# A decoder layer on one core: the self-attention half rebuilt around two heads per pass, masked diagonal blocks and one-bank row maxima

## The chip, the core and the metric

The program runs on 1 core of one Trainium2 chip. The metric is the device time of one execution in microseconds. The engines: TensorE (PE; its weight loads are PEld in the profile) multiplies, VectorE (DVE), ScalarE (ACT) and GpSimd (POOL) compute on rows of 128 partitions, SyncE (SP) issues the DMAs. TensorE writes to PSUM, which has 8 banks of 512 fp32 columns.

## What is computed

One pre-norm decoder layer on x of shape (1, 1024, 128): self-attention, cross-attention to a context of 6404 rows with an added mask, and an FFN with weights and activations rounded to FP4 blocks. Only the self-attention is touched by the change, and the turning of the context that is done on its way:

```python
q = x @ W_q ; k = x @ W_k ; v = x @ W_v
latent_kv = (k + v) @ W_down_kv
k_rec = (latent_kv @ W_up_k)  # 16 heads of 8
v_rec = (latent_kv @ W_up_v)
scores = einsum('bhqd,bhkd->bhqk', qh, k_rec) / sqrt(d)
decay = exp(-0.01 * abs(t[:, None] - t[None, :]))
attn = softmax(scores * decay)
out = einsum('bhqk,bhkd->bhqd', attn, v_rec) @ W_o
```

## The kernel before

All code is written out per engine, with semaphores between the engines; each engine executes its instructions in the order written, so the order of the text is the order of the work.

**Operands.** A head has only 8 dimensions, and the scores are wanted at fp32 accuracy from bf16 matmuls. So each of q and k is split into PARTS = 3 bf16 parts, and 9 products of parts are stacked as 72 rows of one contraction. `|i-j|` in the decay is taken apart: exp(-a(i-j)) is a factor of the query times a factor of the key, right below the diagonal; its inverse is right above it. So there are four operands, QL and KL ("lower"), QU and KU ("upper"). Three more rows (72 to 74) carry minus the row maximum of the query in three parts, against rows of ones. The parts are computed by ScalarE and VectorE, stored to DRAM (`key_parts`, `query_parts`) and loaded back in the stacked form, three loads per operand (`load_operand`, L286 to L296). There are NB = 3 operand buffers for the NG = 4 groups of HG = 4 heads.

**Maxima.** The softmax needs the row maximum before the exponential. One unit is 128 queries of a head against all 1024 keys: two matmuls (`max_unit`, L868 by way of the helper `mm`) into two banks, then one VectorE instruction that multiplies by the decay table and reduces to a maximum (L671). 16 units make a half group (4 heads, 512 queries); 128 units in all. After each half group the 16 columns of maxima are turned on TensorE (`max_rows`, L930), split into three parts on VectorE (`shift_split`, L702 to L705), and written by 6 DMAs into the shift rows of the operand (`load_shift`, L304). Units run ahead of the loop: 16 + MAX_LEAD = 25 are done in a fill before it, and the others go two to a block.

**Scores.** A block is one pair of a query half (512 columns) and two key tiles, 4 heads: four units of 128 keys by 512 queries in banks 0 to 2 in turn. Even units hold a diagonal 128x128 piece, in which neither factor form is right; it is multiplied without shift rows, VectorE multiplies it by the table `diagT` (L747), and TensorE then adds the shift with a matmul against `ones_rows` (`shift_diag`, L958). Odd units are wholly on one side. ScalarE takes the exponential of a unit (L537). P·V is four matmuls side by side, one head in each 32 columns of the array, summing in bank 3 over the 8 blocks of a half group (`pv`, L969). 64 blocks in all. This line sets TensorE's order in a block (s = shift, A and B = a maximum unit each, D, N, d, n = scores):

```python
ORDER = "s0 A D1 PV s1 N1 d0 B n0".split()
```

After every 8 blocks the scores of the next half group wait for its shift rows (`nxt`).

**SyncE** issues in this order: ones, parts of KL and QL, their loads, parts of QU and KU, their loads, then group by group operands and shift rows; the context (`mem`, 3.3 MB, L335 and L336) after two groups; the cross-attention's masks after the last P·V.

**Other work in the loop.** VectorE computes the scales of the FFN weights in blocks 8 to 10 (`weight_scales`). In the last blocks TensorE turns the context (`mem_tiles`, L981) and VectorE splits it into a high and a low part (`mem_parts`, L692 and L694). After the loop comes the cross-attention for 8 tiles of 128 queries, then the FFN, pipelined; they begin at 291 us.

Of the kernel before, what the change touches and what calls it, by code (L numbers as in the profile page):

```python
# [15 lines left out]
P = 128  # L16
# [7 lines left out]
SHIFT_ROW = 72  # L24
MATH_ROWS = 72
FULL_ROWS = SHIFT_ROW + PARTS
HG = 4
# [3 lines left out]
def decoder_layer(nc, x, ctx, mask, w_q, w_k, w_v, w_o, w_down_kv, w_up_k, w_up_v,  # L31
# [27 lines left out]
    MAX_LEAD = 9  # L59
    MEM_BLOCK = (NG * NH * UNITS - UNITS - MAX_LEAD + 3) // 2  # L60
    EARLY_BLOCK = NG * NH * (S // P) - 3
    SCALE_BLOCK = NT
# [4 lines left out]
    with ExitStack() as stack:  # L67
# [8 lines left out]
        SLOTS = 2 * PARTS - 1  # L76

        k_scratch = nc.dram_tensor("key_parts", [2, SLOTS, HD, HEADS, S], BF16, kind="Internal").ap()
# [4 lines left out]
        wq_sb = sb("wq_sb", [P, D]); wk_sb = sb("wk_sb", [P, D]); wv_sb = sb("wv_sb", [P, D])  # L83
        wo_sb = sb("wo_sb", [P, D]); wdn_sb = sb("wdn_sb", [P, DL])
        wuk_sb = sb("wuk_sb", [DL, D]); wuv_sb = sb("wuv_sb", [DL, D])
        xw_sb = sb("xw_sb", [P, D]); xwT = sb("xwT", [P, D]); xb_sb = sb("xb_sb", [P, 1])
        half_neg = sb("half_neg", [P, NT])
        ones_rows = sb("ones_rows", [P, P], BF16)
# [8 lines left out]
        row_max = sb("row_max", [P, NG * NH * UNITS])  # L97
        shift_r = sb("shift_r", [UNITS, 1, P])
        shift_parts = sb("shift_parts", [UNITS, PARTS, P], BF16)
        diagT = sb("diagT", [P, P])  # L100
# [6 lines left out]

        memT_lo = sb("memT_lo", [P, NK * P], F32R)
        qc = sb("qc", [P, 2, P])
# [5 lines left out]
        NB = 3  # L115
        OPW = HG * S
        with ExitStack() as self_stack:
            def sb1(name, shape, dt=F32):
                return self_stack.enter_context(nc.sbuf_tensor(name, shape, dt))
            ops = [sb1(f"operands_{b}", [P, 4, HG, S], BF16) for b in range(NB)]  # L120
            probs = sb1("probs", [P, 2 * HG, BANK])
            oT = sb1("oT", [P, NG * NH, BANK])
            v_ext = sb1("v_ext", [P, NT, HEADS, VW])
            decay = sb1("decay", [P, 2 * S - P])
        OPB = 4 * HG * S // 2
        logits_0 = sb("logits_0", [P, S2])
        pT = sb("pT", [P, 3, BANK]); sb("pad_0", [P, OPB - S2 - 3 * BANK])
        mem = sb("mem", [P, NK, D])
        fa = sb("fa", [P, 4, FF]); sb("pad_1", [P, OPB - NK * D - 4 * FF])
        memT_hi = sb("memT_hi", [P, NK * P], F32R)  # L130
        fb = sb("fb", [P, 4, FF]); sb("pad_2", [P, OPB - NK * D - 4 * FF])
        logits_1 = sb("logits_1", [P, S2]); sb("pad_3", [P, 16 * BANK - S2])
# [5 lines left out]
        def operand(buf, which):  # L138
            return ops[buf][:, which, :, :]
# [4 lines left out]
        def queries(buf, which, half):  # L144
            return ops[buf][:, which, :, :].rearrange("p h n -> p (h n)").rearrange(
                "p (a h n) -> p a h n", a=NH, h=HG)[:, half, :, :]
# [25 lines left out]

        ones_src = xqT[:, 0:P // 2].bitcast(BF16)
        xT = ops[2][:, 2, 0:2, :].rearrange("p h n -> p (h n)").bitcast(F32)
# [3 lines left out]
        scaled = [probs[:, 4, :], probs[:, 5, :]]  # L178
        wq_dh, wuk_dh = probs[:, 6, 0:D], probs[0:DL, 6, D:2 * D]
        wkvT, wdnT = probs[:, 6, 2 * D:3 * D], probs[0:DL, 6, 3 * D:4 * D]  # L180
        w_lift, w_rec = probs[:, 7, 0:2 * D], probs[:, 7, 2 * D:4 * D]
        parts_sb = ops[1][:, 0:PARTS, :, :].rearrange("p w h n -> p (w h) n").rearrange("p (w a) n -> p w a n", w=4)
        iota_i = ops[2][:, 0, 0:4, :].rearrange("p h n -> p (h n)")[:, 0:2 * (2 * S - P)].bitcast(I32)
        iota_d = ops[2][:, 1, 0:4, :].rearrange("p h n -> p (h n)")[:, 0:2 * (2 * S - P)].bitcast(I32)
# [1018 lines left out]
```

## Time and profile before

| | |
|---|---|
| median of 3 runs | 584.27 us (576.2 to 584.42) |
| the profiled execution | 584.69 us, of which the span of the core is 583.0 us |
| mean granted TensorE clock | 0.893 of 2.4 GHz |
| busy: TensorE, VectorE, ScalarE, GpSimd | 504.6, 403.5, 301.2, 102.3 us |
| preparation and fill of maxima | 0 to 66 us |
| self-attention loop | 66 to 291 us |
| cross-attention and FFN | 291 to 583 us |

All times are microseconds in one profiled execution unless another unit is given. An engine's name with "idle before" says how long it stood and whose instruction released it. PEclk is the granted TensorE clock as a share of 2.4 GHz; 0.5 is the lower of its two levels, 1.2 GHz.

### The profile page before, as it was taken

What the parts mean: (1) busy time and instruction counts of PE and PEld (TensorE: products, weight loads), DVE (VectorE), ACT (ScalarE), POOL (GpSimd) and SP (SyncE); (2) the same over time, 40 slices, a digit from 0 to 9 for tenths busy, and PEclk for the clock granted to TensorE, in tenths of its full rate; (3) what the DMA queues carried; (4) which work ended last, traced back from release to release, by engine and by line L of the source; (5) the groups of instructions that cost most, each with busy time, mean ns of one, the idle gap of its engine ahead of it and who ended that gap; (6) DMA issues with size and microseconds to landing.
All of it is one profiled execution on the core that took longest, in us unless ns stands there. A gap on an engine that the chain in (4) does not pass through costs nothing.

```text
span 583.0 us, 9028 instructions
## 1 busy us (share of the span) xinstructions
PE 504.6 (87%) x3222; PEld 321.0 (55%) x3222; DVE 403.5 (69%) x1026; ACT 301.2 (52%) x601; POOL 102.3 (18%) x119
## 2 busy tenths in 40 slices
PE   7258999889999999999887998989899898989953
PEld 6101233223233333345365997978789797878851
DVE  3889869879698988889377345756646566664443
ACT  4710256447475757677716572726446372638420
POOL 6020000980000000000034322221312212210000
PEclk9755579879698989899989998989989998999985
DMA  2690535307000800001057524323232422400000
GB/s 65 191 276 22 102 66 103 65 2 161 5 1 3 226 3 1 3 3 37 1 190 224 146 83 117 115 72 110 87 110 86 146 87 79 139 15 6 1 6 5
DMA packets 20727, 46.04 MB, mean 79 GB/s; under 512 B 4470, under 2 KB 9786, under 8 KB 20106
## 3 DMA queue, kind: packets, MB, share of 16 engines
q1 hardware_dynamic: 19930, 44.74, 27.9%
q8 instruction: 26, 0.43, 0.3%
q0 software_dynamic: 224, 0.54, 0.3%
q10 hardware_dynamic: 528, 0.18, 0.2%
q14 instruction: 19, 0.16, 0.1%
HBM read 40.39 MB, written 4.72 MB: 77 GB/s over the span
## 4 chain that ended last, share of the span: by engine, by line
PE 66%; DVE 25%; issue 3%; DMA 2%; ACT 2%; POOL 0%; SPq 0%; DVEq 0%; ACTq 0%; POOLq 0%
PE banks L868 43%; PE banks L969 11%; DVE banks L671 8%; PE banks L1101 6%; PE banks L958 3%; DVE logits L775 3%; DVE fa L811 1%; DMA operands<-query_parts 1%; DVE qc_lo L729 1%; PE banks L981 1%; DVE fa L810 1%; DVE fa L806 1%; DVE f_small L802 1%; ACT probs L537 1%; DMA x_sb<-in_x 1%
## 5 line engine op out<-in xcount | busy, mean ns | idle before, releaser
L537 ACT ACTIVATE probs<-banks 128x512 f32<-128x512 f32 x256 | 139.1, 596 | 117.4 <-PE banks L958 115.3
L868 PE MATMUL banks<-operands 72*128 72x512 bf16 (+5 forms) x704 | 158.3, 360 | 14.6 <-DMA operands<-query_parts 8.0
L671 DVE CUSTOM_DVE_ANT_0 banks<-banks,decay 128x1024 f32<-128x1024 f32 x128 | 156.5, 1228 | 15.1 <-PE banks L868 11.2
L868 PEld LDWEIGHTS banks<-mem,pT 128*128 128x128 f32 (+1 forms) x816 | 107.9, 195 | 7.7
L868 PE MATMUL banks<-mem,pT 128*128 128x128 f32 (+1 forms) x816 | 111.5, 279 | 0.0
L868 PEld LDWEIGHTS banks<-operands 72*128 72x128 bf16 (+1 forms) x704 | 62.0, 104 | 82.1 <-DVE row_max L671 24.5
L775 DVE CUSTOM_DVE_ANT_0 logits<-banks,mring 128x512 f32<-128x512 f32 (+1 forms) x102 | 67.4, 668 | 46.6 <-PE banks L868 23.2
L559 ACT ACTIVATE pT<-banks 128x512 f32<-128x512 f32 (+1 forms) x104 | 60.4, 581 | 52.6 <-PE banks L1101 52.6
L969 PE MATMUL banks<-probs,v_ext 128*32 128x512 f32 x512 | 76.6, 673 | 0.7 <-ACT probs L537 0.7
L430 POOL TENSOR_SCALAR mring<-mring 128x1024 f32<-128x1024 int32 (+1 forms) x55 | 52.7, 959 | 90.3 <-DMA mring<-in_mask_BxSxS_ik 88.1
L868 PE MATMUL banks<-memT_hi,qc_hi 128*128 128x512 f32 (+1 forms) x104 | 50.4, 485 | 17.7 <-DVE cmax L775 17.7
L1101 PE MATMUL banks<-ident,logits 128*128 128x128 f32 (+1 forms) x408 | 63.5, 279 | 0.0
L549 ACT ACTIVATE logits<-logits,neg_max 128x1024 f32<-128x1024 f32 (+1 forms) x56 | 58.8, 1051 | 6.4 <-DVE neg_max L782 6.4
L958 PEld LDWEIGHTS banks<-operands,ones_rows 75*128 75x128 bf16 x128 | 12.5, 98 | 83.8 <-DVE banks L747 67.9
L747 DVE TENSOR_TENSOR banks<-banks,diagT 128x128 f32<-128x128 f32 x128 | 40.6, 317 | 21.1 <-PE banks L868 21.0
L1101 PEld LDWEIGHTS banks<-ident,logits 128*128 128x128 f32 (+1 forms) x408 | 49.4, 143 | 4.0 <-issue 2.0
L868 PE MATMUL banks<-memT_hi,qc_lo 128*128 128x512 f32 (+1 forms) x104 | 41.4, 398 | 0.0
L868 PE MATMUL banks<-memT_lo,qc_hi 128*128 128x512 f32 (+1 forms) x104 | 41.1, 395 | 0.0
L958 PE MATMUL banks<-operands,ones_rows 75*128 75x128 bf16 x128 | 29.8, 233 | 12.5 <-DVE banks L747 12.3
L420 POOL TENSOR_TENSOR rstd<-mv,half_neg 128x1 f32<-128x1 f32 x16 | 8.8, 552 | 146.3 <-DVE mv L817 83.2
L868 PEld LDWEIGHTS banks<-memT_hi,qc_hi 128*128 128x128 f32 x104 | 20.7, 199 | 20.4 <-DVE cmax L775 19.7
L430 POOL TENSOR_SCALAR mask<-mask 128x1024 f32<-128x1024 int32 x1 | 1.0, 1046 | 135.5 <-DMA mask<-in_mask_BxSxS_ik 135.5
(162 smaller groups left out, 456.0 us busy)
## 6 DMA issues: line engine op xcount, KB each, us to landing
mring<-in_mask_BxSxS_ik SPq DMA_DIRECT2D x47, 512.0 KB, 3.5
operands<-key_parts SPq DMA_DIRECT2D x24, 192.0 KB
operands<-query_parts SPq DMA_DIRECT2D x24, 192.0 KB
key_parts<-operands SPq DMA_DIRECT2D x10, 256.0 KB, 3.5
query_parts<-operands SPq DMA_DIRECT2D x4, 384.0 KB, 4.7
mring<-in_mask_BxSxS_ik SPq DMA_DIRECT2D x8, 130.0 KB, 2.1
operands<-shift_parts SPq DMA_DIRECT2D x48, 4.0 KB, 1.7
x_sb<-in_x SPq DMA_DIRECT2D x1, 512.0 KB, 4.4
```

The costliest lines, as they stand in the source:

```text
L420: pool.tensor_tensor(rstd[:, t:t + 1], mv[:, t, 1:2], half_neg[:, t:t + 1], ALU.pow).then_inc(done, 1)
L430: pool.tensor_scalar(src.bitcast(F32), src, -1.0, -NEG, ALU.add, ALU.mult).then_inc(s_ma, 1)
L537: act.activation(probs[:, (gb % 2) * HG + h, :], PS[:, u % 3, :], ACT.Exp).then_inc(s_p, 1)
L549: act.activation(y, y, ACT.Exp, bias=neg_max[:, t:t + 1], accum_out=esum[:, t, e:e + 1]).then_inc(s_e, 1)
L559: last = act.activation(pT[:, n % 3, 0:o], PS[:, 2 + n % 2, 0:o], ACT.Copy)
L671: dve.tensor_tensor_reduce(out=rows, in0=rows, in1=decay[:, off:off + S], scale=1.0, scalar=-3.0e38, op0=ALU.mult, op1=ALU.max, accum_out= ...
L747: dve.tensor_tensor(PS[:, u % 3, c0:c0 + P], PS[:, u % 3, c0:c0 + P], diagT[:, :], ALU.mult).then_inc(s_dd, 1)
L775: dve.tensor_tensor_reduce(out=logits_sb(t)[:, k0:k0 + kw], in0=PS[:, logits_bank(n), 0:kw], in1=mk, scale=1.0, scalar=-3.0e38, op0=ALU.ad ...
L868: return pe.matmul(o, a, b, start=start, stop=stop)
L958: pe.matmul(PS[:, u % 3, d0:d0 + P], ones_rows[0:FULL_ROWS, :], queries(gb // BLKS % NB, QL, half)[0:FULL_ROWS, h, d0:d0 + P], start=False ...
L969: last = pe.matmul(PS[h * VW:(h + 1) * VW, 3, :], v_ext[:, kt, g * HG + h, :], probs[:, (gb % 2) * HG + i, :], start=(b % NT == 0), stop=( ...
L1101: last = pe.transpose(PS[0:kw, 2 + n % 2, j * P:(j + 1) * P], logits_sb(t)[:, k * P:k * P + kw], ident[:, :])
```

## The change

It rebuilds the self-attention and leaves the mathematics of the cross-attention and the FFN.

1. **Operands.** 6 products of parts in place of 9: 48 rows, then 3 shift rows at 48, in runs given by `RUNS`. Heads h and h+2 of a group lie in the two row halves of the array (rows 0 and 64, `ROW_HALF`), so one slot of work is one matmul per half. Two operand buffers. Loading a group takes 36 DMAs instead of 12.
2. **Diagonal blocks.** The VectorE multiplication and the shift matmul are gone. The lower form is computed over the diagonal piece too; a bf16 matmul of an identity against a table of 0 and -1e30 (`side_mask`) adds -1e30 on the wrong side (L1101). A fifth slot per pair of blocks computes the four heads' diagonal pieces in the upper form, with the other side masked (`diag_scores`, L1114), and its P·V is added apart (`pv_diag`, L1139).
3. **Maxima** from operands of their own (`max_queries`, `max_keys`, 32 rows, four row quarters), in pieces of one bank (512 keys) in a ring of banks 5 to 7: 256 pieces, 44 of them in the fill, then 8 to a pair of blocks. Per piece one VectorE instruction; the two halves of 16 rows' maxima are joined by one more (`join_pieces`).
4. **Shift rows.** GpSimd splits the joined maxima (`max_split`), TensorE turns the three parts at once as bf16 (L1053), ScalarE copies them out (`take_shift`), SyncE writes them with 12 DMAs per half group (L375).
5. **Loop.** 32 pairs of 5 slots. A slot's scores are two banks (0-1 or 2-3), and ScalarE takes one exponential over both (128x1024; 128x512 for the diagonal slot). P·V in two halves of 256 columns, bank 4.
6. **Context.** Loaded right after the weights, turned in the fill (steps from unit 6 on) into banks 0 to 3; ScalarE copies the high part, TensorE subtracts it by a matmul with a negative identity (`mem_rest`), ScalarE copies the low part. VectorE and the loop have none of it.
7. **Parts.** Low parts and the upper operands' remainders move from VectorE to GpSimd, the FFN scales ahead of the first maximum piece.

The diff, cut to its core:

```diff
-SHIFT_ROW = 72
-MATH_ROWS = 72
+ROW_HALF = 64
+RUNS = ((0, 3, 0), (24, 2, 1), (40, 1, 2))
+SHIFT_ROW = 48
...
-    MAX_LEAD = 9
+    SLOTS = 5
+    MAX_LEAD = 6
+    ROWS_LATE = 4
+    FILL = HG_PIECES + MAX_LEAD * NH
...
+            sp.dma_start(mem[:, 0:NKF, :], ctx[0, 0:NKF * P].rearrange("(t p) d -> p t d", p=P)).then_inc(s_mem, 16)
...
+            for i in range(3):
+                weight_scales(i)
...
-                    dve.tensor_tensor(PS[:, u % 3, c0:c0 + P], PS[:, u % 3, c0:c0 + P], diagT[:, :],
-                                      ALU.mult).then_inc(s_dd, 1)
...
+                dve.tensor_tensor_reduce(out=rows, in0=rows, in1=decay[:, off:off + BANK], scale=1.0, scalar=-3.0e38,
...
+            def scores(n, j):
...
+                mm(PS[:, bank + 1, :], keys(g % NB, side[1], h)[:, kt * P:(kt + 1) * P], queries(g % NB, side[0], half, h))
...
+                mm(PS[:, bank, d0:BANK], keys(g % NB, KL, h)[:, ks], queries(g % NB, QL, half, h)[:, d0:BANK])
...
+                pe.matmul(PS[:, bank, d0:d0 + P], ident_b[:, :], side_mask[:, 0, :], start=False, stop=True,
+                          skip_group_check=True).then_inc(s_st, 1)
...
+                        act.activation(probs[:, gb % 2 * HG + i:gb % 2 * HG + i + 2, :],
+                                       PS[:, q % 2 * 2:q % 2 * 2 + 2, :], ACT.Exp).then_inc(s_p, 1)
...
+            pe.wait_ge(s_mlo, NC)
+            for n in range(PAIRS):
+                scores(n, 0)
+                if n > 0:
+                    pv(2 * n - 1, 0)
+                max_turn(8 * n)
+                max_turn(8 * n + 1)
+                scores(n, 1)
...
+                diag_scores(n)
+                pv(2 * n, 1)
+                max_turn(8 * n + 7)
```

**TensorE, one block before**, early in the first group. `ones_rows` with `operands` is the shift matmul, `operands` alone scores or a maximum unit (the unit waits for `max_scores_taken`), `v_ext` P·V:

```order
L958 MATMUL banks<-operands_0,ones_rows 128x128 [waits diag_decayed]
L868 MATMUL banks<-operands_0 128x512 [waits max_scores_taken]
L868 MATMUL banks<-operands_0 128x512
L868 MATMUL banks<-operands_0 128x128 [waits probs_ready]
L868 MATMUL banks<-operands_0 128x256
L868 MATMUL banks<-operands_0 128x128
L969 MATMUL banks<-probs,v_ext 32x512 [waits probs_ready]
L969 MATMUL banks<-probs,v_ext 32x512 x3
L958 MATMUL banks<-operands_0,ones_rows 128x128 [waits diag_decayed]
L868 MATMUL banks<-operands_0 128x512 [waits probs_ready]
```

**TensorE, the last pair before a half group ends, after the change**: from the end of its slot 0 on. `max_keys` is a maximum piece, `qc,xqT` the mask matmul (these two tiles hold the masks and the bf16 identity meanwhile), `xqT,max_parts` the turning of the split maxima:

```order
L1053 MATMUL banks<-xqT,max_parts 48x128 [waits max_scores_taken,max_split]
L1001 MATMUL banks<-max_keys_1,max_queries_1 128x512 [waits max_scores_taken] x2
L1001 MATMUL banks<-operands_0 128x512 [waits probs_ready]
L1001 MATMUL banks<-operands_0 128x128
L1001 MATMUL banks<-operands_0 128x384
L1101 MATMUL banks<-qc,xqT 128x128
L1128 MATMUL banks<-probs,v_ext 32x256 x4
L1001 MATMUL banks<-max_keys_1,max_queries_1 128x512 [waits shift_rows_ready]
...
L1114 MATMUL banks<-qc,xqT 128x256 x2
L1128 MATMUL banks<-probs,v_ext 32x256 x4
L1001 MATMUL banks<-max_keys_1,max_queries_1 128x512 [waits max_scores_taken]
L1001 MATMUL banks<-operands_0 128x512 [waits probs_ready,shift_loaded_1]
```

The scores of the pair after it wait for the shift rows that were turned one pair earlier. Scores, masks, P·V and pieces alternate in each slot; before, a shift matmul and P·V stood among scores.

**SyncE before**, from the first query parts to the operand loads:

```order
L277 DMA query_parts<-operands_1 128x3x512 [waits lo_ready]
L277 DMA query_parts<-operands_1 128x3x512
L296 DMA operands_0<-key_parts 24x4096 [waits scratch_written_1]
L296 DMA operands_0<-key_parts 24x4096 x2
L296 DMA operands_0<-query_parts 24x2x2048 [waits scratch_written_0]
L296 DMA operands_0<-query_parts 24x2x2048 x2
```

**SyncE after**, from the first keys on, the context first; `xqT` is the source of the ones, and `xn` holds the copied shift rows:

```order
L312 DMA mem<-in_ctx_1024 128x50x128 [waits kv_weights_loaded,weights_loaded,x_loaded]
L313 DMA mem<-in_ctx_1024 4x128
L317 DMA key_parts<-operand_parts 128x1024 [waits hi_ready]
L317 DMA key_parts<-operand_parts 128x1024 [waits mid_ready]
L323 DMA query_parts<-operand_parts 128x2x512 [waits mid_ready]
L323 DMA query_parts<-operand_parts 128x2x512
L353 DMA max_keys_0<-key_parts 8x2x512 [waits scratch_written_1]
L353 DMA max_keys_0<-key_parts 8x2x512 x15
L361 DMA max_queries_0<-query_parts 16x2x1024 [waits scratch_written_0]
L361 DMA max_queries_0<-query_parts 16x2x1024 x7
...
L375 DMA operands_0<-xn 1x8x128 [waits shift_rows_ready]
L375 DMA operands_0<-xn 1x8x128 x11
```

The context load now stands ahead of every store of parts, and all of the first group's loads and those of the next group's maxima stand ahead of the first shift rows.

## Rows read from the trace of the kernel before

**Rows 1.** The page's first part: busy us (share of span) xinstructions.

```profile
PE 504.6 (87%) x3222; PEld 321.0 (55%) x3222; DVE 403.5 (69%) x1026; ACT 301.2 (52%) x601; POOL 102.3 (18%) x119
```

**Rows 2.** Stretches: each engine's busy time (instructions), PEclk, DMA share, GB/s.

```profile
0.00:66.00 66.00, 42.25 (x138) 15.56 (x139) 52.06 (x106) 19.27 (x33) 13.17 (x20) 0.66 0.46 130
66.00:80.00 14.00, 13.61 (x53) 4.68 (x52) 8.52 (x18) 6.25 (x12) 0.00 (x0) 0.51 0.73 137
...
102.00:110.00 8.00, 5.44 (x39) 1.87 (x38) 7.79 (x21) 3.78 (x8) 7.42 (x8) 1.00 0.58 119
...
147.00:160.00 13.00, 12.37 (x52) 4.08 (x56) 7.92 (x18) 5.27 (x10) 0.00 (x0) 0.61 0.02 3
160.00:176.00 16.00, 16.00 (x120) 6.23 (x112) 15.37 (x37) 11.92 (x24) 0.00 (x0) 1.00 0.01 2
...
291.00:583.00 292.00, 252.23 (x1735) 224.76 (x1735) 166.07 (x513) 139.90 (x304) 61.01 (x70) 0.94 0.30 91
```

**Rows 3.** TensorE's timeline: start, duration, line, xcount, [idle before <-releaser].

```profile
33.44 1.86 PE L868 MATMUL banks<-operands 72*128 72x512 bf16 x4 [7.96 <-DMA operands<-query_parts]
```

**Rows 4.** SyncE's timeline: DMA issues, as start, duration, line, xcount.

```profile
15.98 2.70 SPq L272 DMA_DIRECT2D key_parts<-operands  x5
...
23.01 2.11 SPq L296 DMA_DIRECT2D operands<-key_parts  x3
...
56.32 3.78 SPq L304 DMA_DIRECT2D operands<-shift_parts  x6
60.15 1.60 SPq L282 DMA_DIRECT2D operands<-xqT  x2
...
93.50 1.18 SPq L296 DMA_DIRECT2D operands<-key_parts  x3
...
189.04 9.36 SPq L336 DMA_DIRECT2D mem<-in_ctx  x1
```

**Rows 5.** TensorE's timeline in an undisturbed block.

```profile
159.62 1.06 PE L969 MATMUL banks<-probs,v_ext 128*32 128x512 f32 x8
...
161.77 0.22 PE L958 MATMUL banks<-operands,ones_rows 75*128 75x128 bf16 x1
161.83 0.82 PE L868 MATMUL banks<-operands 72*128 72x512 bf16 x4
162.57 1.06 PE L969 MATMUL banks<-probs,v_ext 128*32 128x512 f32 x8
163.57 0.23 PE L958 MATMUL banks<-operands,ones_rows 75*128 75x128 bf16 x1
```

**Rows 6.** Groups, 80 to 250 us: xcount | busy us, mean ns | idle before, releaser.

```profile
L671 DVE CUSTOM_DVE_ANT_0 banks<-banks,decay 128x1024 f32<-128x1024 f32 x95 | 116.4, 1226 | 11.3 <-PE banks L868 7.6
L537 ACT ACTIVATE probs<-banks 128x512 f32<-128x512 f32 x191 | 103.8, 596 | 64.4 <-PE banks L958 62.9
...
L747 DVE TENSOR_TENSOR banks<-banks,diagT 128x128 f32<-128x128 f32 x96 | 31.0, 323 | 11.5 <-PE banks L868 11.5
```

**Rows 7.** Waits, 80 to 250 us: who for whom, us, times, longest.

```profile
PEld banks L958 <- DVE banks L747: 52.7, 59, 2.0
```

**Rows 8.** ScalarE's timeline around a handover of shift rows.

```profile
147.90 1.08 ACT L537 ACTIVATE probs<-banks 128x512 f32<-128x512 f32 x2 [1.59 <-PE banks L958]
151.98 1.09 ACT L537 ACTIVATE probs<-banks 128x512 f32<-128x512 f32 x2 [2.99 <-PE banks L958]
```

**Rows 9.** VectorE's timeline in the cross-attention.

```profile
341.12 0.69 DVE L775 CUSTOM_DVE_ANT_0 logits<-banks,mring 128x512 f32<-128x512 f32 x1 [0.28 <-DVE cmax L775]
...
341.74 0.35 DVE L725 TENSOR_SCALAR xn<-x_sb,mv,rstd 128x128 f32<-128x128 f32 x1
```

**Rows 10.** ScalarE's timeline when the small weights have arrived.

```profile
7.59 0.43 ACT L466 ACTIVATE probs<-wuk_sb 32x128 f32<-32x128 f32 x1 [1.13 <-DMA xb_sb<-in_L_xattn_b]
```

**Rows 11.** The tile of split maxima: duration of its DMAs' issue, min/median/max ns, and landing.

```profile
L304 SPq DMA_DIRECT2D operands<-shift_parts x48: 502/589/1372, 56.3 to 260.6; - x48
...
DMA to landing us min/median/max: 1.7/1.7/2.8
```

## What the change should do to the time: the prediction

> **What bounds the kernel now.** I read the page's first part, then a table of stretches, then the waits and the engine timelines inside the self-attention loop. The page alone misleads: TensorE is busy 87% of the span [rows 1], but two different programs share that figure. From 291 us on the kernel is cross-attention with TensorE busy 252 of 292 us [rows 2], and the change leaves that part as it is. So the question is what happens in the first 291 us. These split into a preparation (first matmul of a maximum at 33.44 us, waiting for query operands [rows 3]), a fill of 25 maximum units, and 64 blocks of the loop, from the first exponential at 66 us to the last P·V at 291 us, where I cut the stretches of [rows 2].
>
> In an undisturbed stretch of the loop (160 to 176 us) TensorE is busy all the time and VectorE 15.37 of 16 us [rows 2]; P·V starts at 159.62 and again at 162.57, so a block takes 2.95 us [rows 5]. VectorE ends it: per block two maximum units of 1.23 us and two diagonal multiplications of about 0.32 us [rows 6] make 3.1 us, less some overlap of neighbours. TensorE waits for those multiplications for 52.7 us [rows 7], ScalarE for TensorE's shift matmuls for 62.9 us [rows 6]. 64 x 2.95 = 189 us, yet the loop takes 225. The other 36 us are a cold start (clock 0.51 from 66 to 80 us [rows 2]), the FFN weight scales put among the blocks, and seven handovers of shift rows, after which ScalarE waits 1.59 and 2.99 us and the clock falls: 0.61 over 147 to 160 us [rows 2, 8].
>
> **The change, part by part, for one pair of blocks (5.9 us before without handovers).**
>
> VectorE: the diagonal multiplications and the shift split go. Eight one-bank maxima replace four of two banks. The nearest operation, the masked logits of 128x512 from PSUM, starts at 341.12 and the next instruction at 341.74 [rows 9]: 0.62 us, so 8 x 0.62 = 5.0 us. One join of 128x16 per 32 pieces is nothing beside that.
>
> ScalarE: four exponentials of 1024 columns and one of 512. A 512 one lasts 596 ns, two in a row take 1.08 us [rows 6, 8]; a double one lies between 0.98 (one start saved) and 1.1 us (none saved). I take 1.0: 4.6 us.
>
> TensorE: columns at 2.4 GHz. A 512-column bf16 matmul is 0.213 us. Scores: two heads in two row halves, 0.213 us if they run side by side, plus the mask of 128 columns, 0.053: four slots, 1.07 us. Diagonal slot: 0.11 + 0.21 for the two masks of 256 columns, 0.32. P·V in fp32: two passes of two, 4 x 512 columns = 0.853 us per block whether halved or not: 1.71. P·V of the diagonal parts 0.11 more (a quarter of the columns, half as long each pass). Maxima: eight pieces in five groups, 5 x 0.213 = 1.07 us, since a group of two sits in two row quarters. Together 4.3 us. Side by side is not shown for rows here; for columns it is: the eight records of one P·V last 1.06 us together [rows 5], where one after another they would need 4 x 0.853.
>
> But TensorE changes its tiling between these. The order shows, in each of five slots, scores (51 rows), mask (128 rows), P·V (32 columns), pieces (32 rows): four changes, 20 per pair. The price is in the rows: from the shift matmul at 161.77 to P·V at 162.57 are 0.80 us for 128+512+512+384+128 = 1664 columns, 0.69 us; from P·V at 162.57 to the next at 163.57 are 1.00 us for 0.85 [rows 5]. So about 0.1 us for going in and 0.1 for coming out, though before it happens twice in a block. 20 x 0.1 = 2.0 us: TensorE needs 6.3 us per pair, more than VectorE. With a short wait for the third bank I take 6.4. The bounds: 5.1 (changes free, VectorE sets it) and 8.0 (nothing side by side: 4 x 0.21 + 0.11 + 3 x 0.21 = 1.6 more).
> The Trainium skill says in "TensorEngine Tiling (Array Packing)", Key Properties, that changing the tiling mode, not only the tile, drains TensorE. The trace agrees for a column tiling, at 0.1 us. Were it free for row tilings, the pair would take 5.1 us, and the sum would be near 577.
>
> Pieces end after 26.5 pairs (212 pieces are left after the fill, eight a pair). The last 5.5 pairs lack them and one change per slot: 6.3 - 1.07 - 0.5 = 4.7 us, ScalarE 4.6; I take 4.9. Loop: 26.5 x 6.4 + 5.5 x 4.9 = 197 us.
>
> Start of the loop. SyncE is the path here. The context load is put ahead of everything else: it can be issued when the small weights are in, 7.6 us [rows 10], and a load behind it held SyncE for 9.36 us [rows 4], so SyncE is free at 17.8 us, 2 us after the key parts are there. The stores then follow its 3.3 MB: key and query parts are back at about 23.5 us (23.0 before [rows 4]). From there SyncE issues: 24 loads for the maxima, 8 of ones, 8 stores, 36 operand loads, 24 loads for the maxima of the next group, 12 shift rows. Spacings: loads 0.41 us (three in 1.18 plus the gap), ones 0.80, stores 0.5 (five in 2.70), shift rows 0.63 (six in 3.78) [rows 4]. Sum: 9.8 + 6.4 + 4 + 14.8 + 9.8 + 7.6 = 52.4, and 1.7 for the last to land [rows 11]: 77.5 us. First maximum at 23.5 + 9.8 + 2 = 35.5 us, two later than before. The fill (44 pieces of 0.62 us, from the sixth unit on with 16 steps of transposes and remainder matmuls on TensorE) ends between 62 us (full clock) and 80 us (half clock) and lies beside the queue. I take 77.5, between 70 and 82. ScalarE's 26 copies of 0.6 us, GpSimd's remainders and the scales, now ahead of the first maximum, are covered by the same queue; uncovered, the scales' 5 us would come ahead of the first maximum.
>
> Handovers. The rows of half-group x are turned in slot 0 of pair 4x-1 and wanted by the first scores of pair 4x: one pair, 6.6 us with the transpose. The chain in it: 1.2 us to the transpose, 0.8 to ScalarE's copy behind an exponential, then 12 DMAs, where before there were 6 with four blocks (12 us) of lead, then 1.7 us landing [rows 11]. The nearest row is 0.63 us a DMA with 16 pieces each; these have 8, the loads of long rows take 0.41. I take 0.55: 2.0 + 11 x 0.55 + 1.7 = 9.75, so TensorE stands for 3.1 us (1.6 at 0.41, 4.0 at 0.63). Behind it wait P·V of the last block, then all pieces, so VectorE too; nothing catches up since TensorE bounds. After such stops before, the clock fell for some 3.4 us; TensorE then loses half, 1.7 us. 7 x 4.8 = 34 us.
>
> Sum: 77.5 + 197 + 34 + 292 (from 291 us to the end, unchanged) = 600.5 us of span, + 1.7 for what lies around it (584.69 against 583.0): 602, which I keep, since the median of 584.27 us is only 0.4 below the profiled execution.
>
> **Rivals.** A measurement can tell about 2%, 11.7 us, from no change.
> 1. Faster: the issue of short DMAs is cheaper than any row here (0.3 us or less). Then the queue ends near 68 us, the fill sets 70, the handover chain is 2.0 + 3.3 + 1.7 = 7.0 and hides but for 0.4 us: 70 + 197 + 3 + 292 + 1.7 = 564. For it: each DMA carries half the pieces. Against: 0.589 us is the median of the shift rows, 0.502 the least [rows 11].
> 2. No change: shift rows at 0.41 us and the clock holds through stops of 1.6 us: 75 + 197 + 11 + 292 + 1.7 = 577, with half of the clock drops 583. A free change of tiling comes to 577 as well (34 us less in the pairs, 9 more in the handovers, whose lead is one pair). For it: over 102 to 110 us TensorE was busy 5.44 of 8 us and the clock stayed at 1.00 [rows 2].
> 3. Much slower: the row halves do not run side by side. Pair 8.0 us, last pairs 5.9, stops 1.5 + 1.7: 77.5 + 244 + 22 + 292 + 1.7 = 637. Against: columns do.
>
> **How the numbers follow.** Forecast 0.46, rival 1 0.22, rival 2 0.20, rival 3 0.12. The forecast's own range is 584 to 613 (stops of 1.6 to 4.0 us, loop start 70 to 82). For 8 in 10 the range takes in rival 1 and most of rival 3: 560 to 632. Faster by over 2%: rival 1 and a bit, 0.24. Within 2%: rival 2 and the forecast's lower end, 0.26. Slower: 0.50.
>
> **What would show it.** Right: a pair at 6.3 to 6.6 us with TensorE never idle and VectorE waiting for it; 0.1 us between matmuls of different tilings; scores of heads h and h+2 starting within some 10 ns; SyncE issuing without a pause from 24 to 76 us; at seven places the first scores waiting for DMA operands<-xn, 2 to 4 us. Wrong: pairs at 5 us with VectorE full; shift DMAs under 0.4 us; first exponential before 70 us; two heads' matmuls 0.2 us apart.

## The result, and the profile after

The changed kernel takes 711.15 us (median of 4 runs, 709.95 to 712.27), the kernel before 583.11 us (median of 4); the ratio is 1.2225 with a 95% interval of 1.2123 to 1.2327. The forecast was 602 us, the range ended at 632. The sign was right, the size was not: the time is 109 us above the forecast and 79 us above the end of the range.

The stretches of the changed kernel show where. Columns as in [rows 2].

```profile
0.00:66.00 66.00, 44.13 (x189) 24.20 (x189) 48.83 (x134) 33.13 (x60) 51.85 (x60) 0.77 0.56 162
66.00:77.50 11.50, 0.60 (x1) 0.10 (x1) 2.11 (x8) 0.05 (x1) 4.31 (x6) 0.51 0.16 43
80.00:376.00 296.00, 294.96 (x1806) 71.46 (x1804) 150.67 (x427) 127.51 (x144) 4.97 (x24) 0.50 0.08 21
380.50:387.00 6.50, 4.87 (x61) 1.74 (x59) 0.00 (x0) 4.58 (x5) 0.00 (x0) 1.00 0.02 3
412.00:708.00 296.00, 255.30 (x1779) 226.35 (x1778) 166.99 (x513) 141.83 (x307) 60.88 (x70) 0.94 0.30 90
```

The last row is the cross-attention: from the end of the last P·V (415.5 us, before 292.0) it is 293 us to the end, before 291. So the change left it as it was, and nearly all of the excess is in the loop, from the first exponential at 78.4 to 415.5 us: 337 us, where it was 226. The third row has the cause in it. For 296 us TensorE is busy almost without a gap (294.96 us), and its granted clock is 0.50, the lower level, all that time. Before, the clock was 1.00 in the undisturbed stretches of the loop [rows 2]. It rises in this trace at 380 us; the last maximum pieces were multiplied from 374.4 to 375.0 us. The page's second part shows it at a glance, the busy share and the clock in tenths, 17.7 us a digit:

```profile
PE   7097699999999999999998987989898989898873
...
PEclk9658555555555555555556799999999999999995
```

The first line misleads: TensorE reads 9 in almost every slice of the loop, nothing looks idle. The second tells it.

The pace can be read off ScalarE's timeline. The first exponential of a pair of blocks starts at 132.50 and the next pair's at 143.75: 11.25 us a pair, where 6.4 were forecast.

```profile
132.50 1.02 ACT L689 ACTIVATE probs<-banks 128x1024 f32<-128x1024 f32 x1 [1.72 <-PE banks L1101]
134.82 1.02 ACT L689 ACTIVATE probs<-banks 128x1024 f32<-128x1024 f32 x1 [1.29 <-PE banks L1101]
...
143.75 1.02 ACT L689 ACTIVATE probs<-banks 128x1024 f32<-128x1024 f32 x1 [1.72 <-PE banks L1101]
```

In TensorE's timeline the same work, a slot without pieces, stands at both clocks, first at the lower level and then, after the rise, at the higher:

```profile
376.29 0.60 PE L1001 MATMUL banks<-operands 51*128 51x512 bf16 x3
376.83 0.29 PE L1101 MATMUL banks<-qc,xqT 128*128 128x128 bf16 x1
377.05 1.08 PE L1128 MATMUL banks<-probs,v_ext 128*32 128x256 f32 x8
...
381.24 0.39 PE L1001 MATMUL banks<-operands 51*128 51x512 bf16 x3
381.56 0.23 PE L1101 MATMUL banks<-qc,xqT 128*128 128x128 bf16 x1
381.72 0.64 PE L1128 MATMUL banks<-probs,v_ext 128*32 128x256 f32 x8
382.29 0.39 PE L1001 MATMUL banks<-operands 51*128 51x512 bf16 x3
```

A slot without pieces takes 382.29 - 381.24 = 1.05 us at 2.4 GHz: 0.32 from scores to mask, 0.16 to P·V, 0.57 to the next scores. Its columns alone need 0.213 + 0.053 + 0.427 = 0.69, so three changes of tiling cost 0.36 us, 0.12 each. From 376.29 to 377.05 at 1.2 GHz are 0.76 us for 0.427 + 0.107: two changes, 0.11 each. The change from P·V to what follows is 0.57 - 0.427 = 0.14 at 2.4 GHz and 1.01 - 0.853 = 0.16 at 1.2 GHz (377.05 to 378.06). So a change costs about the same time at either clock.

So the question for the runs: why does a TensorE that is always busy not get its higher clock? Theory A: the content, small tiles that fill too little of the array. Theory B: history, the clock was lost at the wait before the loop (66 to 77.5 us, second row above), and the loop keeps what it has. Theory C: the empty time at the changes of tiling. Theory D: the stops at the handovers of shift rows.

TensorE's timeline shows when the clock was lost: with the last piece of the fill, at 66.2 us, 0.6 us before the long wait began and not in it. A piece takes 0.38 us at 2.4 GHz and 0.60 at 1.2.

```profile
65.58 0.38 PE L1001 MATMUL banks<-max_keys,max_queries 32*128 32x512 bf16 x1
66.22 0.60 PE L1001 MATMUL banks<-max_keys,max_queries 32*128 32x512 bf16 x1 [0.26 <-DVE xn L834]
```

### The profile page after: what moved, and what is told of

Its sections match the earlier page's. It is cut to its first block, busy times and chain, and to the rows that moved or that the text cites. A ratio compares the mean times of both kernels' runs of the same rounds, so it can differ in the third digit from the quotient of the medians.

```text
span 708.2 us, 11123 instructions
## 1 busy us (share of the span) xinstructions
PE 630.6 (89%) x4098; PEld 334.0 (47%) x4098; DVE 372.1 (53%) x1092; ACT 328.3 (46%) x540; POOL 124.5 (18%) x165
## 4 chain that ended last, share of the span: by engine, by line
PE 71%; SPq 11%; DVE 10%; DMA 3%; issue 3%; ACT 1%; POOL 0%; DVEq 0%; ACTq 0%; POOLq 0%
PE banks L1001 41%; PE banks L1128 16%; PE banks L1266 5%; PE banks L1101 4%; SPq L375 3%; PE banks L1139 2%; PE banks L1114 2%; DVE logits L908 2%; SPq L353 1%; SPq L313 1%; SPq L340 1%; DVE fa L944 1%; DMA mring<-in_mask_BxSxS_ik 1%; SPq L361 1%; DVE qc_lo L872 1%
## 5 line engine op out<-in xcount | busy, mean ns | idle before, releaser
L834 DVE CUSTOM_DVE_ANT_0 banks<-banks,decay 128x512 f32<-128x512 f32 x256 | 173.4, 714 | 163.6 <-PE banks L1001 163.6
L689 ACT ACTIVATE probs<-banks 128x1024 f32<-128x1024 f32 x128 | 130.8, 1024 | 152.4 <-PE banks L1101 152.1
L1128 PE MATMUL banks<-probs,v_ext 128*32 128x256 f32 x1024 | 130.2, 601 | 0.3 <-ACT oT L660 0.3
L1001 PE MATMUL banks<-max_keys,max_queries 32*128 32x512 bf16 x256 | 96.5, 585 | 18.4 <-DMA max_queries<-query_parts 16.8
L1001 PE MATMUL banks<-operands 51*128 51x128 bf16 (+3 forms) x480 | 86.9, 425 | 14.2 <-DMA operands<-xn 14.2
L1001 PEld LDWEIGHTS banks<-max_keys,max_queries 32*128 32x128 bf16 x256 | 17.0, 99 | 119.8 <-issue 71.4
L1001 PEld LDWEIGHTS banks<-operands 51*128 51x128 bf16 x480 | 19.9, 103 | 83.4 <-ACT probs L689 44.4
L1101 PEld LDWEIGHTS banks<-qc,xqT 128*128 128x128 bf16 x128 | 13.4, 105 | 50.3 <-issue 50.3
L694 ACT ACTIVATE probs<-banks 128x512 f32<-128x512 f32 x32 | 19.1, 597 | 38.6 <-PE banks L1114 38.6
L834 DVE DVE_READ_ACCUMULATOR2_ANT xn<- 128x1 f32 x256 | 36.5, 143 | 0.0
```

The source lines that it names most:

```text
L689: act.activation(probs[:, gb % 2 * HG + i:gb % 2 * HG + i + 2, :], PS[:, q % 2 * 2:q % 2 * 2 + 2, :], ACT.Exp).then_inc(s_p, 1)
L694: act.activation(probs[:, 2 * HG + n % 2, :].rearrange("p (r n) -> p r n", r=2), PS[:, q % 2 * 2:q % 2 * 2 + 2, 0:H2 * P], ACT.Exp).then_i ...
L834: dve.tensor_tensor_reduce(out=rows, in0=rows, in1=decay[:, off:off + BANK], scale=1.0, scalar=-3.0e38, op0=ALU.mult, op1=ALU.max, accum_o ...
L1001: return pe.matmul(o, a, b, start=start, stop=stop, skip_group_check=alone)
L1101: pe.matmul(PS[:, bank, d0:d0 + P], ident_b[:, :], side_mask[:, 0, :], start=False, stop=True, skip_group_check=True).then_inc(s_st, 1)
L1128: last = pe.matmul(PS[h * VW:(h + 1) * VW, 4, cols], v_ext[:, kt, g * HG + h, :], probs[:, gb % 2 * HG + i, cols], start=(b % NT == 0 and ...
```

## The experiments

**The clock by itself.** A kernel of nothing but matmul sequences.

```diff
+            for i, stretch in enumerate(STRETCHES):
+                pe.wait_ge(s_r, i + 1)
+                stretch(pe, PS, w, m, v, pr).then_inc(s_t, 1)
+                wide(pe, PS, w, m, v, pr)
+                stretch(pe, PS, w, m, v, pr).then_inc(s_t, 1)
```

> Measures TensorE's granted clock by itself; nothing of the layer is computed, the output is a copy of x. Ten kinds of matmul sequence, each twice: first behind a pause of TensorE (about 8 us), then behind 48 matmuls of 128 rows by 512 columns. The kinds, in order: 128 rows; one 32-row quarter at a time; two quarters side by side; four quarters side by side; the scores' two row halves of 51 rows; P-V in four column tiles; the loop's slot (scores, mask, P-V, two pieces); the slot without pieces; the slot with one piece of 128 rows; the slot without mask. Theory A (content: what the loop's matmuls fill of the array is too little for the higher clock): the slot runs at 0.5 both behind the pause and behind the dense stretch, after a few us; one and two quarters too; the slot without pieces and the slot with the 128-row piece rise to 1.0. Theory B (history: any back-to-back stream holds what it has, only the pause before the loop lost the clock): behind the dense stretch every kind stays at 1.0. Theory C (the empty time at changes of tiling counts as rest): all four slot kinds stay at 0.5, but one, two and four quarters alone, which have no change of tiling, rise to 1.0.

Stretches of its TensorE (columns: PE and PEld busy, ACT, POOL, then PEclk): the loop's slot behind a pause; the loop's slot behind the dense matmuls; the slot without pieces behind a pause, before and after the clock rose; the slot with a 128-row piece, the same two; the slot without mask behind a pause.

```profile
226.40:254.40 28.00, 27.78 (x168) 6.60 (x170) 0.00 (x0) 0.00 (x0) 0.50 0.01 1
267.20:283.00 15.80, 15.80 (x165) 5.28 (x164) 0.00 (x0) 0.00 (x0) 1.00 0.00 1
290.40:295.80 5.40, 5.40 (x39) 1.35 (x39) 0.00 (x0) 0.00 (x0) 0.50 0.01 3
296.00:305.40 9.40, 9.33 (x107) 3.30 (x107) 0.00 (x0) 0.00 (x0) 1.00 0.00 0
335.60:339.60 4.00, 3.53 (x24) 0.91 (x25) 0.00 (x0) 0.00 (x0) 0.50 0.00 0
342.00:353.00 11.00, 10.49 (x103) 3.67 (x105) 0.00 (x0) 0.00 (x0) 1.00 0.01 1
388.10:413.00 24.90, 24.90 (x156) 5.13 (x154) 0.00 (x0) 0.00 (x0) 0.50 0.00 1
```

The bare slot, with no other engine and no DMA in play, shows the fault: behind a pause it stays at 0.50 for its whole 28 us; behind the dense stretch it has 1.00 for its whole 16 us. Without pieces it rises after 5.6 us, with a 128-row piece after 4.8. Without the mask, which is one change of tiling less per slot, it doesn't rise in 25 us. Four row quarters side by side, the row halves and the four column tiles, each alone, all rose within 5 us. So did two quarters, 3.5 us into their stretch:

```profile
73.97:77.50 3.53, 3.53 (x36) 1.39 (x40) 0.00 (x0) 0.00 (x0) 0.50 0.00 0
77.50:81.00 3.50, 3.50 (x68) 1.44 (x61) 0.00 (x0) 0.00 (x0) 1.00 0.02 5
```

The 48 pieces in successive quarters took 5.28 us at 1.2 GHz, where one after the other they need 20.5 (they ran side by side), and the clock rose just as they ended. So 32-row pieces by themselves don't keep the clock low, as theory C had it and theory A had not. No theory stood as it was written: A missed this and that the slot holds the clock once it has it; B missed that the slot can't get it back; C missed that the slots without pieces and with a 128-row piece rise.

**The entry of the loop.** Dense matmuls in the wait ahead of it, and then also in the waits for shift rows.

```diff
             pe.wait_ge(s_mlo, NC)
+            for _ in range(ENTRY_FILLER):
+                mm(PS[:, 4, :], ident_b[:, :], max_k[0][:, 0, :])
             for n in range(PAIRS):
```

> The changed kernel with 50 dense matmuls (128 rows x 512 columns, into the empty bank of P-V) put in the wait before the loop, so that it enters the loop at 2.4 GHz. Theory A (content): the clock falls within some us of the loop's start and the time stays near 711 us. Theory B (history): the clock holds to the first handover of shift rows at least: first pairs at 6.6 us instead of 11.25; if it then falls for good at the first stop, 4 pairs are won, 18 us: 693.

> As warm_entry, and 10 dense matmuls more in each of the seven waits for shift rows. Theory A (content): still near 711 us, clock 0.5 in the pairs with pieces. Theory B (history): the clock holds through the loop, pairs near 6.6 us: 711 - 26.5 x 4.6 + stops of some 3 us = about 600 us.

Measured: 706.95 and 650.88 us (one run each), beside 581.5 for the kernel before. With the filler at the entry alone the clock was 1.00 from 70 us to 83.4, 4 us into the loop, and then at 0.5 to 380. That is theory A's number, yet the same filler in warm_all carried the clock through the first four pairs. With filler in the stops too:

```profile
80.00:114.00 34.00, 31.55 (x277) 11.92 (x275) 21.96 (x65) 18.82 (x21) 0.83 (x4) 1.00 0.15 38
116.00:159.00 43.00, 43.00 (x264) 11.02 (x257) 21.99 (x63) 18.27 (x21) 0.83 (x4) 0.50 0.06 17
160.00:257.00 97.00, 91.05 (x868) 34.77 (x866) 66.40 (x195) 57.92 (x66) 2.50 (x12) 1.00 0.10 27
260.00:302.00 42.00, 42.00 (x256) 10.76 (x255) 21.59 (x61) 17.48 (x20) 0.83 (x4) 0.50 0.10 27
```

Two long stretches at either level, each change at a stop for shift rows, and in between this run's loop keeps what it has: it loses the clock at 114.9 us, gets it back only from the filler of a stop 44 us later, holds it for 99 us. At 1.00 a pair takes 6.8 us, at 0.50 it takes 11.2.

**Wide pieces.** The edit is made for the pieces of the loop alone. This run's shift is not the row maximum (see the expectation), the rest is computed as before.

```diff
-                   max_q[g % NB][r:r + MAX_ROWS, qt // TPB, h % H2, qt % TPB * P:(qt % TPB + 1) * P],
-                   max_k[g % NB][r:r + MAX_ROWS, h % H2, :]).then_inc(s_mx, 1)
+                   max_q[g % NB][:, qt // TPB, h % H2, qt % TPB * P:(qt % TPB + 1) * P],
+                   max_k[g % NB][:, h % H2, :]).then_inc(s_mx, 1)
```

> The changed kernel with the pieces of the loop (not those of the fill) contracted over all 128 rows of the same operand tiles instead of one quarter, scaled by 0.1; so the shift is another number than the row maximum. Same number of pieces, columns and changes of tiling; no two pieces side by side. Theory A (content): the clock rises to 1.0 in the loop, pair 6.6 + 3 x 0.21 = 7.3 us, 711 - 27 x 4 = about 605 us. Theories B and C: the clock stays at 0.5, pair 11.25 + 3 x 0.43 = 12.5 us, 711 + 34 = 745 us.

Measured: 647.6 us (one run). The pair took 7.4 us (7.3 expected) and the mean clock from 82 to 340 us was 0.91. After each stop for shift rows it was at 0.50 for 3.4 to 13.7 us and rose by itself. More TensorE work, 64 us less time. The clock rose by itself at the entry too, 4 us after the first exponential. Most of the excess over 605 is the stops: pairs across a handover took about 11.3 us and those behind them 9 to 11.

**Grouping, rows, length.** The bare slot again, with the same matmuls in another order.

```diff
+        for _ in range(group):
+            scores(pe, PS, w, m)
+        for _ in range(group):
+            one(pe, PS[:, 0, 0:P], w[:, :], m[:, 0:P])
+        for _ in range(group):
+            last = pv(pe, PS, v, pr)
+        for _ in range(group):
+            last = pieces(pe, PS, w, m, quarters, rows)
```

> As modes: nothing of the layer is computed, each kind of sequence once behind a pause and once behind 48 dense matmuls, now with the same two row quarters (0 and 1) for every pair of pieces. In order: the loop's slot 24 times; the same matmuls with two slots' parts side by side (half the changes of tiling); with four slots' (a quarter of them); the slot with both pieces in row halves of 64; the slot with a lone piece; the slot 72 times. Theory A (content of the array alone): regrouping changes nothing, both stay at 0.5 behind the pause; the pieces of 64 rows rise to 1.0; the lone piece rises less readily than the two. Theory C (empty time at the changes of tiling, which is longest against the work there): grouping by two or by four rises to 1.0, pieces of 64 rows too (one change less per slot). Both: the slot behind the dense stretch holds 1.0 for its 72 slots (some 100 us), since at 2.4 GHz nothing stops it.

Stretches: grouped by two, low and then high; grouped by four, the same; pieces in row halves, the same; the lone piece; the loop's slot 72 times behind a pause, and behind dense matmuls.

```profile
105.40:110.00 4.60, 4.60 (x34) 1.52 (x32) 0.00 (x0) 0.00 (x0) 0.50 0.01 4
111.00:134.00 23.00, 23.00 (x288) 9.08 (x284) 0.00 (x0) 0.00 (x0) 1.00 0.01 1
180.30:185.00 4.70, 4.70 (x40) 2.31 (x42) 0.00 (x0) 0.00 (x0) 0.50 0.01 3
185.50:205.00 19.50, 19.50 (x264) 9.57 (x260) 0.00 (x0) 0.00 (x0) 1.00 0.00 1
250.00:253.50 3.50, 3.50 (x26) 0.89 (x23) 0.00 (x0) 0.00 (x0) 0.50 0.00 0
254.00:270.00 16.00, 16.00 (x182) 5.84 (x178) 0.00 (x0) 0.00 (x0) 1.00 0.00 1
330.20:390.00 59.80, 59.80 (x323) 14.50 (x324) 0.00 (x0) 0.00 (x0) 0.50 0.00 1
438.50:580.00 141.50, 141.50 (x857) 32.99 (x855) 0.00 (x0) 0.00 (x0) 0.50 0.00 1
600.00:700.00 100.00, 100.00 (x988) 34.09 (x989) 0.00 (x0) 0.00 (x0) 1.00 0.00 1
```

This is the run that speaks for C: the same matmuls with half the changes of tiling get the higher clock 4.9 us behind the pause, with a quarter of them 5.1 us behind it, and with the pieces in row halves 3.7 us; ungrouped they ran 143 us without it, and with a lone piece 60 us. That they never get it is too strong: in the 72-slot stretch it rose at 581 us by itself, near its end, and the 24 slots at the start of this kernel went from a slot of 2.31 us to one of 1.37 after 34 us. (The clock column can't be used there: over 8 to 41.5 us it reads 1.00 while the slots take the 2.31 us of the lower level.) After such spans the 28 us of the slot and the 25 us of the slot without mask in the run above are too short to say that those never rise.

**Fewer DMAs for the shift rows**: four of three rows each, the columns of the split maxima reordered for it.

```diff
-                    for i in range(PARTS):
-                        for r in range(2):
-                            top = r * ROW_HALF + SHIFT_ROW + i
+                    for r in range(2):
+                        top = r * ROW_HALF + SHIFT_ROW
...
+                        u0 = r * PARTS * H2 * TPB
+                        sp.dma_start(rows, shift_rows[u0:u0 + PARTS * H2 * TPB, hg % 2, :]).then_inc(s_sh[hg % 2], 16)
```

> The changed kernel with the shift rows written by 4 DMAs per half group of three rows each instead of 12 of one. The chain to the next half group is then 2.0 + 3 x 0.63 + 1.7 = 5.6 us, less than a pair at either clock. Theory A or C (the loop cannot raise the clock by itself): stops go (about 7 x 0.8 us) and the loop starts 5 us earlier, but the clock stays at 0.5 until the pieces end: about 700 us. Theory D (the stops at the handovers are what keeps the clock low): without them it rises within the first pairs: about 590 us.

> Both: 4 DMAs per half group, and 30 dense matmuls in what is left of the wait before the loop. If the clock is lost only where TensorE pauses, it holds from the entry through all 32 pairs: loop start 73, 26.5 x 6.8 + 5.5 x 5.1 = 208 us, and 292 + 1.7 after it: about 575 us, 1.5% under the kernel before. If the slot loses the clock by itself now and then, between that and 700.

> four_dmas_warm timed in rounds: if the clock holds by itself once it is high, all runs lie near 582 us; if it is lost in some (the entry is a matter of luck, as warm_entry was), single runs lie towards 700.

Measured: 697.52 us for four_dmas (one run, the kernel before beside it 585.88); from 67 to 370 us all at 0.50, the pairs 11.2 to 11.5 us, no stop between them. So theory D is out: the stops don't keep the clock low.

```profile
67.00:370.00 303.00, 297.33 (x1817) 72.07 (x1817) 153.46 (x435) 129.40 (x145) 8.37 (x29) 0.50 0.09 23
```

With the filler at the entry the same kernel took 582.42 us (575 expected), its 215 us of loop all at 1.00:

```profile
71.00:286.00 215.00, 210.25 (x2127) 74.44 (x2125) 148.50 (x438) 149.67 (x171) 7.54 (x31) 1.00 0.13 34
```

The same file again gave 699.08, 702.31, 701.96 and 584.98 us: nothing between. In the first of these the clock was at 1.00 from 55 to 79 us and was lost 4 us into the loop, as in warm_entry:

```profile
80.00:370.00 290.00, 290.00 (x1785) 70.16 (x1777) 147.47 (x417) 125.21 (x141) 5.11 (x25) 0.50 0.08 20
```

One program, two times 117 us apart. The mean granted clock was 0.73 to 0.74 in the three long executions and 0.94 in the two short ones. In the traces (two that lost the clock, here and in warm_entry, and two that kept it, four_dmas_warm and warm_all) it is decided in the first pair. In that pair P·V is still missing from three slots. Why it survives in some runs and not in others is open.

**Pieces in the row halves.** The loop's pieces come from the scores' own lower operands, 48 rows, heads h and h+2 side by side; the 32-row operands are loaded for the first group only.

```diff
+                if mp >= FILL:
+                    mm(PS[:, max_bank(piece_turn(mp)), :], queries(g % NB, QL, hg % NH, h)[0:SHIFT_ROW, j * P:(j + 1) * P],
+                       keys(g % NB, KL, h)[0:SHIFT_ROW, i * BANK:(i + 1) * BANK]).then_inc(s_mx, 1)
```

> four_dmas, and the pieces of the loop taken from the scores' lower operands (48 rows, heads h and h+2 side by side in the two row halves) in place of the 32-row operands, whose loads for later groups go; a slot has then three changes of tiling instead of four. No filler. Theory C (what keeps the clock low is the empty time at the changes together with the small tiles; a slot with fewer of them raises the clock by itself, as in modes2): the clock rises in the first pairs, pair 6.8 - 5 x 0.11 = 6.25 us, loop start near 66 us, 66 + 26.5 x 6.3 + 28 + 292 + 2 + some 20 us of half clock at the start = about 570 us. If the whole loop, unlike the bare slot, still can't raise it: near 680 us.

> half_rows with 20 dense matmuls in what is left of the wait before the loop: the clock holds from the entry, 555 to 565 us; only a few us below half_rows if that raises the clock by itself.

Measured: 576.07 us (570.75 to 579.91), ratio to the kernel before 0.9854 (0.9731 to 0.9977); with filler 576.05 us, ratio 0.9894 (0.9822 to 0.9967). Both are 1 to 1.5% under the kernel before, which is within the 2% that counts as no change: the first reads as unclear, the second as the same. The filler gave nothing (555 to 565 us were expected with it): it delays the first exponential from 69.8 to 76.1 us, and that is what it saves in half clock. Without it the clock rises by itself at 87.9 us and stays until the pieces have ended:

```profile
68.00:87.00 19.00, 18.68 (x108) 4.85 (x112) 12.40 (x36) 9.10 (x10) 4.08 (x6) 0.50 0.31 84
88.00:250.00 162.00, 159.41 (x1714) 56.47 (x1711) 134.40 (x401) 119.15 (x136) 4.97 (x24) 1.00 0.09 22
```

A pair takes 6.4 us, 0.4 less than with 32-row pieces at 2.4 GHz: five changes of tiling less were to give 0.55. Its slot, from scores and pieces to the same of the next: 128.24 to 129.51, 1.27 us.

```profile
128.24 0.61 PE L1001 MATMUL banks<-operands 48*128 48x512 bf16 x4
128.78 0.23 PE L1109 MATMUL banks<-qc,xqT 128*128 128x128 bf16 x1
128.94 0.64 PE L1136 MATMUL banks<-probs,v_ext 128*32 128x256 f32 x8
129.51 0.61 PE L1001 MATMUL banks<-operands 48*128 48x512 bf16 x4
```

**Two parts of it undone**: 12 DMAs again, and pieces over 33 rows in the same tiling (their maxima lack part of the products).

```diff
-                    mm(PS[:, max_bank(piece_turn(mp)), :], queries(g % NB, QL, hg % NH, h)[0:SHIFT_ROW, j * P:(j + 1) * P],
-                       keys(g % NB, KL, h)[0:SHIFT_ROW, i * BANK:(i + 1) * BANK]).then_inc(s_mx, 1)
+                    mm(PS[:, max_bank(piece_turn(mp)), :], queries(g % NB, QL, hg % NH, h)[0:MAX_ROWS + 1, j * P:(j + 1) * P],
+                       keys(g % NB, KL, h)[0:MAX_ROWS + 1, i * BANK:(i + 1) * BANK]).then_inc(s_mx, 1)
```

> half_rows with the 12 DMAs of the change for the shift rows: the price of the handovers at 2.4 GHz. By the prediction's chain (2.0 to the copy, 11 DMAs of 0.63, 1.7 to land, against a pair of 6.4) a stop is some 4 us and the clock falls for 3.4 us more; if this loop raises the clock again by itself, 7 x (3.5 to 5.5) = 25 to 40 us above half_rows, 600 to 615 us. If a stop leaves it at 0.5 for long, up to 690.

> half_rows with the loop's pieces contracted over 33 rows instead of 48 (so their maxima lack part of the products): as few rows as the changed kernel's 32, but still one change of tiling less per slot. Theory C (the empty time at changes decides): the clock rises by itself, 576 us as half_rows. Theory A (the rows that the pieces fill decide): it stays at 0.5, near 680 us.

Measured: 645.44 us (643.02 and 647.86) with 12 DMAs, against 576.07. Of the 69 us, 5.4 are the later start (first exponential at 75.2 us instead of 69.8); the other 64 are the seven stops, 9 us each, where 25 to 40 us in all were expected. TensorE stands for 4.2 to 4.5 us in six of them and for 1.5 in the last, 28 us together; the rest goes with the half clock, which holds for 6.8 to 34.1 us at each. Here are one such stop and the longest stretch of half clock:

```profile
110.65 0.61 PE L1001 MATMUL banks<-operands 51*128 51x512 bf16 x2 [4.20 <-DMA operands<-xn]
...
285.00:318.00 33.00, 32.91 (x218) 8.39 (x218) 14.45 (x41) 15.87 (x18) 0.83 (x4) 0.50 0.01 1
```

With 33 rows: 610.76 and 640.96 us. In the first of these, the one with a trace, the clock stayed at 0.50 from 68 to 174 us, then rose and held:

```profile
69.00:173.00 104.00, 103.69 (x662) 26.55 (x665) 57.89 (x166) 47.84 (x54) 5.35 (x13) 0.50 0.12 32
174.00:300.00 126.00, 122.30 (x1332) 43.46 (x1330) 90.74 (x271) 93.83 (x108) 5.18 (x21) 1.00 0.07 19
```

Neither A nor C had this. With 48 rows and one change less per slot the clock rises in 20 us; with 33 rows and the same changes it takes 106 us in one run; with 32 rows and four changes it did not rise in any of the loops of after, warm_entry, four_dmas and four_dmas_warm_b (290 us and more). Both the rows of the pieces (modes and wide_pieces: 128 rows for 32, the changes as many) and the changes of tiling (modes2: the same matmuls grouped) count. Why they do isn't shown.

## Why the prediction was wrong

**What held.** The working of the parts came out nearly as forecast.

- Start of the loop: forecast 77.5 us, set by SyncE's queue. The first scores are at 77.54 us, and wait for the shift rows; the first piece is at 35.09 (forecast 35.5). SyncE issues almost without a pause:

```profile
24.12 5.42 SPq L353 DMA_DIRECT2D max_keys<-key_parts  x16
...
33.20 6.20 SPq L330 DMA_DIRECT2D operands<-xqT  x8
...
68.17 8.15 SPq L375 DMA_DIRECT2D operands<-xn  x12
...
77.54 0.61 PE L1001 MATMUL banks<-operands 51*128 51x512 bf16 x2 [10.72 <-DMA operands<-xn]
```

- The pair at 2.4 GHz: forecast 6.4 us, measured 6.8 in four_dmas_warm. The last pairs: forecast 4.9, measured 5.1 in that run where nothing else came in, but 6.0 across the last handover and 6.4 at the end, where matmuls of the next part stand among theirs. The exponential over two banks: 1.0 and 1.02 us. A change of tiling: 0.1 and 0.11 to 0.16, and this holds now for row tilings too, as the drain that the Trainium skill states in "TensorEngine Tiling (Array Packing)", Key Properties.
- The row halves and quarters run side by side, so rival 3 is out: two records of scores or pieces start within 7 ns of each other, and its 637 us, though nearest to the result, had another mechanism.
- Rivals 1 and 2: a shift DMA takes 0.634 us in the median (x96), as in the rows before, not 0.55 or 0.3.

**Handovers: right mechanism, mis-sized.** Forecast "TensorE stands for 3.1 us" and "the clock fell for some 3.4 us", 4.8 us a handover. At 2.4 GHz, in half_rows_12, TensorE stood for 4.2 to 4.5 us (the forecast's own bound at 0.63 us a DMA was 4.0) and the clock was down for 6.8 to 34.1 us: 9 us each. In the loop of before the clock fell for 3.4 us four times, for 6.8 once, and behind the stop at 148 us for 10.2, which is what 0.61 over 147 to 160 us in [rows 2] says; the forecast took the shortest. In the changed kernel itself they cost little, pairs of 11.5 to 12.1 us beside 11.25, since at half clock the pair is long enough to hide most of the chain.

**The step that failed** is the first sentence on TensorE: "columns at 2.4 GHz". Every column and every 0.1 us of change was priced at the higher clock for the whole loop. I had seen the clock fall at stops and come back, and took it that a TensorE that is never idle has the higher clock. The Trainium skill points the same way in "TensorE: Matmul & The Clock Gate", Part 1, that the default state is throttled and activity releases it; the trace disagrees as far as activity is read as the busy share: 294.96 us busy in 296 and the clock at 0.50. What the runs show in place of it: the clock was lost just before the loop, with the last piece of the fill, stayed low while TensorE waited 10.7 us for shift rows, and this loop, with four changes of tiling in a slot and pieces of 32 rows, mostly can't regain it but can hold it. 26.5 pairs x (11.25 - 6.4) = 128 us; off go some 28 us for six handovers of about 0.5 us and one of 3 instead of seven of 4.8, and 2 us for the first pair, which takes only 8.8; and the last pairs took 9 us or so more, in part since the stop at 385 us cost the clock once more, from 387 to 397 us. That makes about 107; the loop (337 us) exceeds its forecast (197 + 34 = 231) by 106. The same program at the two clocks (four_dmas_warm_b, 585 and 699 to 702 us) shows this price by itself. That the sign came out is partly luck: the forecast's slowdown was to come from the later start, which came, and from the handovers, which cost 6 us here instead of 34.

The row that could have warned stood in the prediction: 66 to 80 us of the kernel before, clock 0.51, TensorE busy 13.61 of 14 us [rows 2]. Its loop too began low and busy, and needed 14 us to get the clock (79.6 us). The prediction called it "a cold start" and charged the new loop nothing for how long such a start may last. With a rival "the clock does not come back" the working was at hand: a pair is 8.6 us of columns at 1.2 GHz plus 20 changes of 0.1 to 0.15, so 10.6 to 11.6 us, and 77.5 + 26.5 x 11.1 + 5.5 x 5 + 292 + 1.7 = about 693 us.

## What to carry to other kernels

Read the granted clock beside the busy share, and price a rebuilt TensorE loop at both clocks: at 1.2 GHz small row tiles and frequent changes of tiling can be a trap that a busy engine doesn't leave. Group matmuls of one tiling, let small products share the tiling of their neighbours (here 48-row pieces in the scores' halves, with the loads that they save: 697 us became 576), and look for the place at which the clock is lost. A time that jumps between two values from run to run, like 585 and 702 here, is a sign of it.

## What the runs showed of the hardware that was not expected

- A sequence can hold the higher clock for 100 us and more and yet stay at the lower one for 143 us, the same matmuls in the same order; only what came before differs.
- Making the pieces do four times the rows, one after the other instead of two side by side, made the kernel 64 us faster (711 to 647.6, one run).
- A change of tiling costs about 0.11 to 0.16 us at either clock, so at 1.2 GHz it doesn't double as the columns do.
- Pieces of 32 rows alone, two row quarters at a time, got the higher clock 3.5 us into their stretch; the slot that mixes them with three other tilings ran 143 us without it.
- Four DMAs of 24 pieces each took 0.70 us apiece to issue, twelve of 8 pieces 0.63 each: in the time to issue it is the number of DMAs that costs, hardly their pieces.
